# A new slot table, a shift row made by VectorE, and PSUM banks split 2 and 3 instead of 3 and 2, in a hybrid attention kernel

## The reference

```python
x = x + attn_a(layernorm(x))       # 16 heads, softmax(q k^T / 4) v, biases
x = x + ffn(layernorm(x))          # gates = sigmoid(q @ routers.T), 255 nodes
x = x + attn_b(layernorm(x))       # rotary, causal
x = x + ffn(layernorm(x))
# ffn: leaf_prob = product of branch probabilities over 8 levels, 256 leaves
#      (leaf_prob @ leaf_values) @ Wout_w.T + Wout_b
```

## Time and profile before

| | us |
|---|---|
| three runs | 1306.0, 1309.14, 1311.37 |
| median | 1309.14 |
| the profiled execution, its own time | 1311.34 |
| its span, first to last instruction | 1309.6 |
| TensorE busy, share of the span | 1169.9 (89%) |
| VectorE busy | 936.4 (72%) |
| ScalarE busy | 718.1 (55%) |
| GpSimd busy | 336.9 (26%) |

### The profile page before, as it was taken

How to read it: one execution, slowest core, us unless ns; L and a number is a source line. 1 busy time by engine, 2 the same in 40 slices (tenths; PEclk the granted TensorE clock), 3 DMA queues, 4 the chain that set the end, 5 groups by cost and what they waited for, 6 DMA issues and landing times.

```text
span 1309.6 us, 19252 instructions
## 1 busy us (share of the span) xinstructions
PE 1169.9 (89%) x6416; PEld 565.2 (43%) x6416; DVE 936.4 (72%) x2599; ACT 718.1 (55%) x1458; POOL 336.9 (26%) x386
## 2 busy tenths in 40 slices
PE   5799999998998989989899998989889898888986
PEld 3123344344443544345343453435444354444544
DVE  3767786857777758876787667886768867787743
ACT  3165755655465555665556555565545665464551
POOL 3011203313241121412315113240323316262220
PEclk9599999999898989999899998999989999998997
DMA  7250310312004130131302213032120402011000
GB/s 204 50 129 1 88 27 17 113 50 73 25 25 121 33 90 10 43 103 33 98 1 83 64 49 81 2 113 66 48 50 2 145 17 86 13 46 53 18 17 17
DMA packets 60977, 75.33 MB, mean 58 GB/s; under 512 B 6064, under 2 KB 46672, under 8 KB 60880
## 3 DMA queue, kind: packets, MB, share of 16 engines
q1 hardware_dynamic: 58768, 73.81, 20.2%
q0 software_dynamic: 2112, 0.30, 0.1%
HBM read 12.45 MB, written 4.19 MB: 13 GB/s over the span
## 4 chain that ended last, share of the span: by engine, by line
PE 59%; DVE 16%; ACT 6%; issue 6%; SPq 5%; DMA 4%; POOL 2%; POOLq 0%; DVEq 0%
PE ps_work L1170 16%; PE ps_out L1087 11%; PE ps_max L1031 9%; PE ps_key L1063 9%; PE ps_work L1196 8%; SPq L447 5%; PE ps_work L1141 4%; DVE ps_max L789 4%; DMA q_stack<-q_part 3%; ACT probs L700 2%; DVE neg_max L793 2%; DVE scratch L944 2%; DVE scratch L947 2%; DVE scratch L916 2%; PE ps_work L1097 2%
## 5 line engine op out<-in xcount | busy, mean ns | idle before, releaser
L700 ACT ACTIVATE probs<-ps_key 128x512 f32<-128x512 f32 (+3 forms) x1024 | 503.9, 518 | 349.7 <-PE ps_key L1063 342.4
L1031 PE MATMUL ps_max<-k_stack,q_stack 96*128 96x512 bf16 (+3 forms) x1024 | 358.0, 357 | 68.0 <-DVE neg_max L789 37.9
L793 DVE TENSOR_REDUCE neg_max<-ps_max 128x1 bf16<-128x512 f32 x512 | 328.9, 683 | 85.8 <-PE ps_max L1031 84.5
L1063 PE MATMUL ps_key<-q_stack,k_stack 97*128 97x512 bf16 (+3 forms) x1024 | 354.7, 350 | 23.2 <-ACT probs L700 14.2
L789 DVE CUSTOM_DVE_ANT_0 ps_max<-ps_max,mask_b 128x128 f32<-128x128 f32 (+3 forms) x512 | 245.6, 504 | 125.9 <-PE ps_max L1031 125.7
L1087 PE MATMUL ps_out<-probs,v_ones 128*32 128x512 f32 (+3 forms) x2048 | 244.4, 550 | 0.6 <-POOL probs L601 0.6
L1031 PEld LDWEIGHTS ps_max<-k_stack,q_stack 96*128 96x128 bf16 x1024 | 101.2, 99 | 324.5 <-DVE neg_max L789 91.7
L1063 PEld LDWEIGHTS ps_key<-q_stack,k_stack 97*128 97x128 bf16 x1024 | 101.3, 99 | 148.1 <-ACT probs L700 74.5
L601 POOL TENSOR_SCALAR_AFFINE_SELECT probs<-probs 128x512 f32<-128x512 f32 x128 | 83.7, 654 | 293.8 <-ACT probs L700 293.4
L587 POOL DMA_DIRECT2D q_stack<-shift_rows x64 | 34.7, 543 | 404.8 <-DVE shift_rows L803 320.5
L1141 PE MATMUL ps_work<-ident,scratch 128*128 128x128 f32 x384 | 63.3, 297 | 26.2 <-DMA a_v_bias<-in_a_v_bias 9.7
(11 more groups left out here) (86 smaller groups left out, 1290.4 us busy)
## 6 DMA issues: line engine op xcount, KB each, us to landing
k_stack<-k_part SPq DMA_DIRECT2D x48, 256.0 KB
q_stack<-q_part SPq DMA_DIRECT2D x48, 256.0 KB
k_stack<-k_part SPq DMA_DIRECT2D x96, 128.0 KB
q_stack<-q_part SPq DMA_DIRECT2D x96, 128.0 KB
x_in<-in_x SPq DMA_DIRECT2D x8, 512.0 KB, 4.7
x_again<-in_x SPq DMA_DIRECT2D x8, 512.0 KB, 4.6
x_moved<-x_plain SPq DMA_DIRECT2D x7, 512.0 KB, 3.3
out<-x_causal SPq DMA_DIRECT2D x7, 512.0 KB, 3.2
```

The source lines that it names most:

```text
L700: act.activation(probs[step % RING][:, j, q0:T], ps_key[slot % 2][:, 0:T - q0], ACT.Exp, scale=SCALE).then_inc(on["exp_done"], 1)
L793: dve.tensor_reduce(out=dst, in_=src, axis=AX_X, op=ALU.max, negate=True)\
L1031: pe.matmul(dst[:, 0:keys], q_stack[n % 2][0:SPLIT_ROWS, h, P * qt:P * qt + P], k_stack[n % 2][0:SPLIT_ROWS, h, 0:keys], start=True, stop= ...
L1063: pe.matmul(ps_key[slot % 2][:, 0:T - q0], k_stack[n % 2][0:STACK_ROWS, h, P * kb:P * kb + P], q_stack[n % 2][0:STACK_ROWS, h, q0:T], star ...
```

## The change

`SCORE_BANKS` goes from 3 to 2 and the work banks from 2 to 3; the sum stays eight. The shift row is transposed by VectorE, which turns `neg_max` (now 128x32, zeros beyond column 16) in blocks of 32x32 to `shift_rows` (now 128x32), and is sent by four DMAs of SP's queue in place of one of GpSimd's. `ident_b` and its events fall away. The tables give matmuls slots of their own: a row is (step, i, slots of its matmuls, slot of the other engines), and a step with two slots has half its matmuls in each. There is one `FINISH` table. Moments, normalization and transposes of a phase move up into the phase before the one that makes its q and k (slots 37 to 55), except for phases 1, 3 and 15 (`ready_late`), where all of them stand at slot 0. `load_x` goes for phase n+2 at slot 10; both `values` steps come in the phase before. `turn_out` moves one slot on. Of the tables a few rows stand for all.

```diff
@@ -31,6 +31,7 @@
 GROUP = 4
 GROUPS = HEADS // GROUP
 COLS = 32
+BLOCKS = P // COLS
 VALUE = DH + 1
 
 
...
@@ -53,9 +54,10 @@
 SHIFT_LAG = 2
 MIX_LAG = 8
 OUT_LAG = MIX_LAG + 1
-TURN_LAG = MIX_LAG + 4
+TURN_LAG = MIX_LAG + 5
 RING = 4
-SCORE_BANKS = 3
+SCORE_BANKS = 2
+WORK_BANKS = 3
...
-FINISH_EARLY = (
...
-    (23, "normalize", 0), (26, "normalize", 1), 
...
+FINISH = (
...
+    ("project_out", 0, (18, 19), 20), ("moments", 0, (), 21),
+    ("project_out", 1, (21, 22), 23), ("moments", 1, (), 23), ("spread", 0, (), 24),
+    ("normalize", 0, (), 27), ("normalize", 1, (), 28),
...
+PREPARE = (
...
+    ("heads_k", 0, (1, 2), 3), ("heads_k", 1, (3, 5), 6), ("heads_q", 0, (6, 7), 8), ("heads_q", 1, (10, 11), 12),
...
 )
...
+def work_of(n):
+
+    if n > 0:
+        yield from ((slots, slot, step, i, n - 1) for step, i, slots, slot in FINISH)
+    for m in range(max(n + 1, 1), min(n + 3, PHASES)):
+        for step, i, slots, slot in PREPARE_CAUSAL if causal(m) else PREPARE_PLAIN:
+            slots, slot = [(max(at, 0) if ready_late(m) else at) + SLOTS * (m - 1 - n) for at in slots], \
+                (max(slot, 0) if ready_late(m) else slot) + SLOTS * (m - 1 - n)
+            if 0 <= slot < SLOTS:
+                yield slots, slot, step, i, m
+
+
 def schedule(n):
 
     due = {}
-    if n > 0:
-        for slot, step, i in FINISH_EARLY if causal(n) and not (n + 1 < PHASES and causal(n + 1)) else FINISH_LATE:
-            due.setdefault(slot, []).append((step, i, n - 1))
-    for m in (n, n + 1):
-        if 0 < m < PHASES:
-            for slot, step, i in PREPARE_CAUSAL if causal(m) else PREPARE_PLAIN:
-                if slot // SLOTS == n + 1 - m:
-                    due.setdefault(slot % SLOTS, []).append((step, i, m))
+    for _, slot, step, i, m in sorted(work_of(n), key=lambda w: w[1]):
+        due.setdefault(slot, []).append((step, i, m))
+    return due
+
+
+def matmul_schedule(n):
+
+    due = {}
+    for slots, _, step, i, m in sorted(work_of(n), key=lambda w: w[1]):
+        for part, slot in enumerate(slots):
+            due.setdefault(slot, []).append((step, i, m, part))
     return due
 
...
                 if out_due(n, slot) is not None:
                     uses.append(("turn_out", n, slot))
-                uses += [(step, i, m, n) for step, i, m in schedule(n).get(slot, ()) if step in BANK_STEPS]
+                uses += [(step, i, m, n) for step, i, m, part in matmul_schedule(n).get(slot, ()) if part == 0]
     uses.append(("turn_out", PHASES, 0))
     uses += [(step, i, PHASES - 1, PHASES) for step, i in FINISH_LAST if step in BANK_STEPS]
-    return {use: at % 2 for at, use in enumerate(uses)}
+    return {use: at % WORK_BANKS for at, use in enumerate(uses)}
 
 
...
         probs = [sb(f"probs{i}", [P, GROUP, T]) for i in range(RING)]
         out_raw = [sb(f"out_raw{i}", [P, T]) for i in range(2)]
-        neg_max = [sb(f"neg_max{i}", [P, TILES, GROUP], BF16) for i in range(2)]
-        shift_both = sb("shift_rows", [COLS + GROUP, T], BF16)
-        shift_rows = [shift_both[COLS * i:COLS * i + GROUP, :] for i in range(2)]
+        neg_max = [sb(f"neg_max{i}", [P, COLS], BF16) for i in range(2)]
+        shift_rows = [sb(f"shift_rows{i}", [P, COLS], BF16) for i in range(2)]
         inverse = sb("inverse", [P, TILES, GROUP])
...
+            def send_shift(n, slot):
+                n, unit, g, _, _ = score_unit(n, slot)
+                if not shift_due(n, unit):
+                    return
+                n, g = (n, g - 1) if g else (n - 1, GROUPS - 1)
+
+                sp.wait_ge(on["shift_row"], count.next("shift_row"))
+                sp.nop(nofuse=True)
+                sent = on["shift_sent0"] if g % 2 == 0 else on["shift_sent1"]
+                row = q_stack[n % 2][SHIFT_ROW:STACK_ROWS, GROUP * g:GROUP * (g + 1), :]
+                row = row.rearrange("o j (t b q) -> o (j t) b q", t=TILES, b=BLOCKS)
+                for b in range(BLOCKS):
+                    sp.dma_start(row[:, :, b, :], shift_rows[g % 2][COLS * b:COLS * b + GROUP * TILES, :])\
+                      .then_inc(sent, DMA)
+
             def core(n, slot):
+                send_shift(n, slot)
                 if slot == 0:
                     if n > 0:
 
                         count.add("keyed_full", SLOTS)
-                    if n + 1 < PHASES and not causal(n + 1):
-                        load_x(n + 1)
+                    else:
+                        load_x(1)
+                if slot == 10 and n + 2 < PHASES and not causal(n + 2):
+                    load_x(n + 2)
                 if slot == 40 and not causal(n):
                     load_again(n)
...
                     count.add("stored")
 
             def opening():
+                for slot in range(-LEAD, 0):
+                    send_shift(0, slot)
...
                     keys = P * (qt + 1) if causal(n) else T
 
                     dve.wait_ge(on["scores_full"], count.next("scores_full"))
-                    src, dst = ps_max[score_bank(n, unit)][:, 0:keys], neg_max[g % 2][:, qt, j:j + 1]
+                    src, dst = ps_max[score_bank(n, unit)][:, 0:keys], neg_max[g % 2][:, TILES * j + qt:TILES * j + qt + 1]
                     if causal(n):
...
+                    count.add("max_done")
                 if shift_due(n, unit):
-                    h, bank = (g + 1) % 2, bank_of["turn_max", *at]
+                    h = (g + 1) % 2
                     sent = on["shift_sent0"] if h == 0 else on["shift_sent1"]
 
-                    dve.wait_ge(on["shift_full"], count.next("shift_full"))
+                    dve.wait_ge(on["max_done"], count.of("max_done", SHIFT_LAG + 1 if n < PHASES else 0))
                     if count.some(f"shift_sent{h}"):
                         dve.wait_ge(sent, count.of(f"shift_sent{h}") * DMA)
-                    count.add(f"shift_sent{h}")
-                    dve.tensor_copy(shift_rows[h], as_rows(bank)).then_inc(on["shift_row"], 1)
+                    count.add(f"shift_sent{h}", BLOCKS)
+                    dve.transpose(shift_rows[h][:, :], neg_max[h][:, :]).then_inc(on["shift_row"], 1)
 
...
-                    last = pe.transpose(as_rows(bank)[:, P * qt:P * qt + P], neg_max[g % 2][:, qt, :], ident_b[:, :])
-                last.then_inc(on["shift_full"], 1)
-
             def ahead(n, slot):
-                at = n, slot
                 n, unit, g, j, qt = score_unit(n, slot)
                 if n < PHASES:
                     scores(n, unit, g, j, qt)
-                if shift_due(n, unit):
-                    turn_max((g - 1) % GROUPS, SHIFT_LAG + 1 if n < PHASES else 0, bank_of["turn_max", *at])
 
             def by_key(n, slot):
...
 
-                    pe.wait_ge(sent, count.next(f"shift_sent{g % 2}") * DMA)
+                    count.add(f"shift_sent{g % 2}", BLOCKS)
+                    pe.wait_ge(sent, count.of(f"shift_sent{g % 2}") * DMA)
 
                 if count.some("exp_done", 1):
...
@@ -1089,9 +1100,9 @@
                                      tile_position=(0, COLS * j))
                 last.then_inc(on["mixed_done"], 1)
 
-            def turn_out(g, bank):
-
-                pe.wait_ge(on["out_ready"], count.of("out_ready"))
+            def turn_out(g, begun, bank):
+
+                pe.wait_ge(on["out_ready"], count.of("out_ready", begun))
                 take(bank, "attended")
                 for qt in range(TILES):
                     last = pe.transpose(bank[:, P * qt:P * qt + P], out_raw[g % 2][:, P * qt:P * qt + P], ident[:, :])
@@ -1100,7 +1111,7 @@
             def core(n, slot):
                 ahead(n, slot)
                 if out_due(n, slot) is not None:
-                    turn_out(out_due(n, slot), bank_of["turn_out", n, slot])
+                    turn_out(out_due(n, slot), 1, bank_of["turn_out", n, slot])
                 by_key(n, slot)
                 if slot % GROUP == MIX_LAG % GROUP:
...
-            def rows(turned, weight, i, bank, width, read):
-
-
-                pe.wait_ge(on["turned"], count.of("turned"))
-                take(bank, read)
-                for t in range(2):
+            def rows(turned, weight, i, bank, width, read, parts, full):
+
+                if 0 in parts:
+                    pe.wait_ge(on["turned"], count.of("turned"))
+                    take(bank, read)
+                for t in parts:
                     tile = slice(P * (2 * i + t), P * (2 * i + t + 1))
                     for k in range(KC):
                         last = pe.matmul(by_tile(bank)[:, t, 0:width], turned[:, k, tile], weight[:, k, 0:width],
                                          start=(k == 0), stop=(k == KC - 1))
-                return last
-
-            def project_out(m, i, n, bank):
-                rows(turned_block, weights["b_o" if causal(m) else "a_o"], i, bank, D, "x_ready")\
```

156 lines of the change are left out of this document (74 added, 82 removed).

## The result

The changed kernel takes 1316.32 us against 1308.2, medians of 20 runs each: a ratio of 1.0061, 95% interval 1.0039 to 1.0083. The forecast was 1277 and 79% for faster.

What follows compares the result with a forecast made beforehand. No engine is full; the order of work bounds the kernel, TensorE and VectorE being crowded in different four-slot windows. 1309.6 - 77 - 13 + 17 + 22 + 5 + 14 = 1277.6 of span, median 1277, range 1236 to 1307.

Steps and rivals of the forecast that it cites:

- tables: Slot tables with steps in halves, all 16 phases: more even engine load, -77 us, from 1209 to 1132 in the sum.
- stacks: Query stack at the start of a phase: its last part ends earlier, so a 13.1 us wait goes, -13 us.
- late phases: Phases 1, 3 and 15, with transposes right behind moments and normalization in slot 0: gaps of 6, 7 and 4, +17 us.
- banks: Two score banks for three: TensorE may be only two maxima ahead, +14 us, bounds 0 and 28.
- VectorE's transpose: The shift row, 64 times: 0.19 us each on VectorE; TensorE loses its 0.41, at most 26 of the 77 us.
- The shift on SP's queue: Shift due in slot 26 of phases 4 to 12 queues behind stack copies, keep and move: 4.5 us late five times, +22.
- elsewhere: Shifts outside those five places: 5.3 us of path against 7.1 of slots, only phases 0, 15 and opening shorter, +5 us.
- Rival (d): Levelling does not pay, as ScalarE's exponentials and two key banks hold the pace: 50 us fall to 15, 1309; chance 0.05.
- Rival (a): Everything is covered: SP keeps up, two banks suffice, only late phases and opening cost, 1242; chance 0.22.
- Rival (c): Shift late in every group, landing 5.0 us: 1.5 late 64 times, 1373, or 1335 at 0.9; chance 0.12.
- The third work bank gets nothing: Work banks going from two to three: no gain, since half steps hold a bank longer and use it up.
- window sum: Dearer of TensorE and VectorE per four-slot window, added: 75.8 us for a new plain phase, 69.7 causal, 145.5 a pair.

Runs made afterwards that it cites:

- the fastest kernel: The changed kernel with the shift made two slots sooner, keep and move in slot 34, three score banks and two work banks: 1224.66 us, ratio 0.9372.

## Why the prediction was wrong

With the banks of the change the runs make a chain of three steps, of which the first holds five terms:

| step | forecast | measured |
|---|---|---|
| tables, stacks, late phases, banks; shift as before (-77 + 26 - 13 + 17 + 14) | 1276 | 1277.0 |
| VectorE's transpose, the row in time (-26) | 1250 | 1246.1 |
| the row late on SP's queue (+22 + 5) | 1277 | 1316.3 |

The first step's forecast is 1309 - 33. The second measurement is the kernel with keep and move at slot 34 and the shift two slots sooner; keep and move at slot 34 are worth nothing alone, so that this step is the transpose. Its 31 has an interval of some 7 on either side. What failed is the step "**The shift on SP's queue**" with its "elsewhere" of 5: a term of 27 us that measures 70 (45 by `keep` and `move` at slot 34 alone, 37 by the two slots alone, 70 by both). At slot 32 the mechanism was right and named with its place, and under-sized. For the rest the 5 us had a landing of 1.7 us and a free queue, and neither held. The other two steps miss by 1 and 5, but that the first is so near is luck: with the old banks the tables give 11 us less than forecast, and the new banks then cost 10 less.

Two sums of the prediction are off as well. 20.1 less 15.8 is 4.3 and not 4.5, which leaves the 22 nearly as it is. Rival (d), 50 of evenness fallen to 15, comes to 1312 and not 1309, so all of it lay above the range.

**Why 70.** *At slot 32:* 4.5 us five times was forecast, 37.6 in all were measured. The path came out at 21.2 us (710.94 to 732.18) for a forecast 20.1: `keep` landed after 8.0 instead of 5.9, the rest was a little shorter. TensorE took 15.2 us over slots 20 to 31 (709.3 to 724.5) instead of 15.8. Half of the excess is that I let `high_q`'s first copy start with slot 20, while it started 1.6 us later. The `keep` of 5.9 came from the kernel before, where SP had issued twelve copies in 8.26 us and then paused for 1.2; now 22 copies go from 701.79 to 717.99, and `keep` 0.16 us behind them. By the Trainium skill, "DMA: Bandwidth & Descriptors", section Queues, rings and completion order, the DMAs that one engine issues share a row of rings, whose descriptors are consumed in order, and this trace is in line with it: a 512 KB copy takes 3.4 us in the median as `move` and 7.6 as `keep`, behind the stacks. It does not show by itself that the order of the ring is the cause and not the bytes in flight.

*Elsewhere:* I compared 5.3 us of path with 7.1 of slots and gave 5 us, taking the queue as free after slot 23. I had worked out what stands ahead of one of four shifts and not of the other three. The shift of slot 10 has six copies ahead of it in phases 3 to 11, and is from 2.5 to 3.3 us late. With the 3.0 us at slot 32 of phase 13 that is 17.5 us. But SP came to the row only 0.7 us late in phase 9; the larger part is the landing, 3.6 us after the last issue instead of 1.7. With the tables alone, one DMA on GpSimd's queue took 5.7 us to land at the same place. So what the forecast lacked here is less the order of the queue than the bytes in flight, whatever queue the shift is on. How the 17.5 us divide between the two was not measured apart. The remaining 10.6 us of the 65.7 are six waits under 1.1 us and two of some 3, at slot 32 of phase 2 and slot 48 of phase 15.

*Behind each wait:* the clock. The mean is 0.935 with all the waits and 0.955 without. Against the changed kernel, 33.9 us less of waits for the row bring 45 us (keep and move at slot 34), 27.8 bring 37 (two slots sooner), 55.3 bring 70 (both; 62.8 to 7.5): 1.3 times the length. From one of these kernels to the next it is 1.2 (28.9 to 7.5 brings 25, 35.0 to 7.5 brings 34). It holds only where nothing else moves: on GpSimd's queue the waits halved and no time came back. The clock behind a wait is a part of it. An estimate from the two windows shown, in which TensorE was busy throughout: 3.8 us at 0.57 lose 1.6 us behind a wait of 7.5, and 4.0 us at 0.50 lose 2.0 behind one of 2.4. By these two the loss goes by the number of waits rather than by their length.

*Rival (a)*, all covered, gave 1242. The kernel in which nearly all is covered (7.5 us of waits for the row), with the same tables and banks, measures 1246: it was a good forecast of another order of the queue. *Rival (c)*, the shift late in every group, overstates: 19 of 64 are late, but the mean over all 64 is 1.0 us, and (c) decides at 0.5. Its landing of 4.0 us or more did come, up to 5.2, but in few groups, the longest of them while stack copies were in flight. Its 12% was too little. I had argued that "after slot 23 little else moves on the queue", true and beside the point for slot 10.

**The banks.** +14 was near the 19 of this kernel and is not a constant. The lost score bank costs 31 on the kernel before, 4 with the tables alone (not clear of nothing), 5 with keep and move at slot 34, 19 on the changed kernel and 21.5 once the shift is in time (1246.1 against 1224.7). "The third work bank gets nothing" is wrong for the tables alone, where the cost of the pair of changes nearly vanishes and the waits for a work bank with it.

**The tables.** With three score banks the tables alone make 1273 where my terms give 1262, a miss of 11 with an interval of 7 on either side. With the shift in time the phases come out near the window sum: 75.3 for 75.8 and 65.5 for 69.7 in the fastest kernel, 67.1 to 69.2 in the odd phases from 3 to 13 with the shift two slots sooner. But these kernels have the new transpose too. By the tables alone levelling was worth some 40 us of the forecast 51 (36 gained, less the 13 of the stacks, plus the 17 of the late phases, both as forecast). That refutes rival (d) with its 15, and leaves the sum somewhat too high.

**The transposes.** 26 us for four transposes leaving TensorE came out as 31 with two score banks and three work banks (1277.0 to 1246.1), which is not clear of 26, and as 48 with three and two (1272.9 to 1224.7). A likely reason for the difference is that there each turn of the shift also took one of only two work banks: the 25.4 us of waits above. It was not tested by itself.

**The rest.** The wait for the query stack went, as forecast. The gaps of the late phases are 6.7, 8.8 and 4.6 us for a forecast 6, 7 and 4. VectorE's transpose takes 204 ns for 190.

## What to carry to other kernels

A DMA that one engine waits for goes to a queue on which nothing late or large stands ahead of it, and its landing is costed by what is in flight on all queues at that moment, not by the median (here 1.6 us against 5.7). When it is moved, the whole order of the new queue is written out for every one of its instances, not for the worst, with the real start of each path. Cost a wait above its length (here 1.2 to 1.3 times), part of it for the clock that falls behind it. And look for the slack that a change makes possible (here two slots, free once TensorE was out of the path) before giving up on the change: the new tables and the new transpose, with the shift, `keep` and `move` placed otherwise on one queue and the old banks, are 6.3% faster where the change was 0.6% slower.
